# Moving the next pass's conditioning products and the home of S2 in a TensorE-filled kernel

## What is computed

```
W = weights[condition]                       # (64, 64, 64), one matrix per batch element
y = einsum('bct,bcd->bdt', x, W)             # the conditioning product
scores = y @ Wr.T                            # (4096, 64)
top_vals, top_idx = top_k(scores, 16)
G = zeros(4096, 64) with softmax(top_vals) at top_idx
h = einsum('nd,krd->nkr', y, A)              # (4096, 64, 16)
out = einsum('nkr,kdr->nd', h * G, B) * 2.0
return x + out
```

## Time and profile before

| | us |
|---|---|
| median of 3 runs | 730.85 |
| the runs | 730.23 to 731.08 |
| the profiled execution | 730.23 |
| its span in the profile | 728.4 |
| PE (TensorE matmul) busy | 714.4 (98%) |
| DVE (VectorE) busy | 490.7 (67%) |
| ACT (ScalarE) busy | 261.7 (36%) |
| POOL (GpSimd) busy | 51.0 (7%) |

### The profile page before, as it was taken

The page is one execution under the profiler, slowest core; times in us unless marked ns, Lnnn a source line. Parts: engine busy times, 40 slices in busy tenths (PEclk is TensorE's granted clock), DMA queues, the critical chain, the costliest instruction groups (busy, mean ns, idle before and its releaser), DMA issues.

```text
span 728.4 us, 9257 instructions
## 1 busy us (share of the span) xinstructions
PE 714.4 (98%) x3440; PEld 599.6 (82%) x3440; DVE 490.7 (67%) x945; ACT 261.7 (36%) x498; POOL 51.0 (7%) x38
## 2 busy tenths in 40 slices
PE   8999989999999999999999999999999999999998
PEld 7877767788888888888888888888888888888886
DVE  4598899997544787856434569875544386887742
ACT  4658662452423543222331544213222255223200
POOL 0683800000000000000000000000000000000000
PEclk9999999999999999999999999999999999999999
DMA  9949339965796956576678586746666777545663
GB/s 317 409 183 319 125 138 390 360 246 217 274 302 228 344 191 238 179 253 245 227 255 297 198 301 234 260 174 235 214 248 246 274 271 278 187 160 185 224 227 144
DMA packets 56158, 178.41 MB, mean 245 GB/s; under 512 B 9650, under 2 KB 9778, under 8 KB 55602
## 3 DMA queue, kind: packets, MB, share of 16 engines
q1 hardware_dynamic: 53954, 172.78, 65.2%
q10 hardware_dynamic: 2160, 5.05, 2.0%
HBM read 131.66 MB, written 46.14 MB: 244 GB/s over the span
## 4 chain that ended last, share of the span: by engine, by line
PE 87%; DVE 12%; ACT 0%; issue 0%; POOL 0%; DVEq 0%; POOLq 0%
PE Pb L266 40%; PE Pb L248 35%; PE Cb L228 6%; PE S L282 4%; DVE Cq L364 2%; DVE Wt L199 2%; DVE Op L181 2%; DVE R L364 1%; PE T L510 1%; DVE Xo L181 1%; DVE Q L364 1%; DVE BR L364 1%; PE T L299 0%; PE T L354 0%; DVE u L364 0%
## 5 line engine op out<-in xcount | busy, mean ns | idle before, releaser
L248 PE MATMUL Pb<-Op,Wt 128*128 128x512 f32 x1008 | 239.0, 392 | 6.9 <-DVE Op L181 5.1
L248 PEld LDWEIGHTS Pb<-Op,Wt 128*128 128x128 f32 x1008 | 187.4, 188 | 46.9 <-DVE Op L181 6.8
L266 PE MATMUL Pb<-Wt,Op 128*128 128x512 f32 x912 | 212.9, 391 | 2.6 <-DVE Op L181 2.6
L266 PEld LDWEIGHTS Pb<-Wt,Op 128*128 128x128 f32 x912 | 169.8, 188 | 38.3 <-DVE Op L181 3.9
L364 DVE TENSOR_TENSOR Q<-Pb,Q 128x512 f32<-128x512 f32 x112 | 77.4, 691 | 89.9 <-PE Pb L266 89.8
L266 PE MATMUL Pb<-Wt,Ox 128*128 128x512 f32 x432 | 100.8, 391 | 0.0
L234 ACT COPY R<-Cb 128x512 f32<-128x512 f32 x60 | 35.2, 586 | 169.5 <-PE Cb L228 169.4
L266 PEld LDWEIGHTS Pb<-Wt,Ox 128*128 128x128 f32 x432 | 80.5, 188 | 16.3
L181 DVE TENSOR_TENSOR Op<-R,Op 128x512 fp32r<-128x512 f32 x98 | 71.3, 752 | 19.0 <-ACT Op L179 19.0
L364 DVE TENSOR_TENSOR Cq<-Pb,Cq 128x512 f32<-128x512 f32 x64 | 44.1, 689 | 40.9 <-ACT Cq L375 30.9
L248 PE MATMUL Pb<-Ox,Wt 128*128 128x512 f32 x288 | 66.3, 389 | 0.0
(11 more groups left out here) (87 smaller groups left out, 482.6 us busy)
## 6 DMA issues: line engine op xcount, KB each, us to landing
Wt<-Wd SPq DMA_DIRECT2D x168, 512.0 KB, 4.8
Wd<-Wt SPq DMA_DIRECT2D x56, 512.0 KB, 3.9
Q<-in_x SPq DMA_DIRECT2D x32, 512.0 KB, 5.0
xc<-in_x SPq DMA_DIRECT2D x24, 512.0 KB, 4.4
out<-Q SPq DMA_DIRECT2D x32, 256.0 KB, 2.5
out<-Q SPq DMA_DIRECT2D x16, 512.0 KB, 2.8
BR<-in_x SPq DMA_DIRECT2D x12, 256.0 KB, 10.3
BR<-in_B SPq DMA_DIRECT2D x3, 1024.0 KB, 9.4
```

The lines of the kernel that those rows point to most:

```text
L248: t = pe.run(lambda e, c=c, o=o, a=a, z=z: e.matmul(Pb[:, b, :], Wt[:, k, a, 128 * c:128 * c + 128], part(o, z), start=fresh and (c, a, z) ...
L266: t = pe.run(lambda e, c=c, o=o, k=k, a=a, z=z: e.matmul(Pb[:, b, :], part(o, a)[:, 128 * i:128 * i + 128], Wt[:, k, z, :], start=fresh an ...
```

## The change

Three things change, all in pass 0. The tiles of the next pass's conditioning product stand behind other steps of the second half (`SPREAD`). S2 lies in `xc`, not in the upper half of `R[:, 1]`. With that the waits follow: "D" waits for the last use of the `Xo` slots, not for the earlier readers of R; the ScalarE copies of tiles 4 to 7 no longer wait for `S2_split`; and the first two loads of `xc` are issued at the steps 14 and 16 of the second half behind `S2_split`, not at the steps 24 and 26 of the first. The passes 1 to 3 keep their order.

```diff
-SPREAD = [1, 3, 4, 7, 16, 18, 20, 22]
+SPREAD = [18, 19, 21, 22, 23, 25, 26, 27]
...
-        S2x = [R[:, 1, 4 + c, :] for c in range(4)]
+        S2x = [xc[:, c // 2, 512 * (c % 2):512 * (c % 2) + 512] for c in range(4)]
...
             to = R[:, i // 4, 4 * a:4 * a + 4, 128 * (i % 4):128 * (i % 4) + 128]
-            ac.after(t, R_free[0], *(S2_split if i >= 4 else ()))
+            ac.after(t, R_free[0])
...
-                    if more and step in (24, 26):
-                        k = (step - 24) // 2
-                        if s == 0:
-                            xc_free[k] = op_free[NO + 4 + k]
-                        load_x(s + 1, k)
+                    if s and more and step in (24, 26):
+                        load_x(s + 1, (step - 24) // 2)
...
                         raw["D", j] = add(ve, s2_place(j), Cq[:, 1, j, :], Cq[:, 3, j, :], Cq_ready[1][j], Cq_ready[3][j],
-                                          *((u_busy[j],) if s else (split["y22"][j][1], t2[j], t3[j])), op=ALU.subtract)
+                                          u_busy[j] if s else op_free[NO + 4 + j // 2], op=ALU.subtract)
...
                     elif more:
                         split.setdefault("next", []).append(operand(y21[c], R_ready[0][1]))
+                    if s == 0 and step in (14, 16):
+                        xc_free[(step - 14) // 2] = S2_split[step - 13]
+                        load_x(1, (step - 14) // 2)
                     b, done = second(base + 28 + 4 * m, split[uses[m]], i, i == 3, name not in CHAIN)
```

## The result

| | before | changed |
|---|---|---|
| median, us | 730.45 (6 runs) | 736.9 (6 runs) |
| the runs, us | 729.66 to 731.08 | 736.41 to 738.64 |
| span of the profiled execution, us | 728.4 | 735.4 |
| time of the profiled execution, us | 730.23 | 737.22 |

The ratio to before is 1.0092, with a 95% interval of 1.0082 to 1.0102. 737.7 was predicted, in a range of 735.9 to 740.3.

A forecast was written before the change was run, and what follows sets the result against it. VectorE sets the pace until 152 us, TensorE after. Span 728.4 + 7.12 = 735.5 us, other terms 0; with 1.83 us around it 737.35, or 737.97 by the median. Predicted 737.7, range 735.9 to 740.3.

The forecast's parts named there:

- SPREAD, steps 0 to 8: Pass 0's second half: VectorE's times stay, TensorE waits more, step 8 restarts at 152.04 with four tiles (7.12 us) less done.
- SPREAD, steps 8 to 27: Rest of that half, at TensorE's pace with eight tiles instead of four: ends at 219.0, not 211.91; +7.12 us.
- ScalarE in the late steps: Tile copies ahead of the next splits in late steps: parts ready in time, term 0; outer end 0.5 us once.
- D's wait: First D, pass 0: new wait over beforehand, old one may have cost something; term 0, 0.4 us either way.
- Loads of xc: Late steps: median landing 5.6 us fits the 7.2 us windows of tiles 4 and 7; term 0, outer end +5.7 us.
- The signs of being wrong: S2's operand 3 over 1 us before 151.3, matmuls waiting for an xc load, or granted clock of 137 to 160 below 1.00.
- Rival (a), a hidden gain: Early steps: without tiles ScalarE runs ahead, VectorE's waits vanish, 728.2 us; 3 in 100, partial gain another 5.
- Rival (c), the clock: TensorE's clock halves for a step behind the long waits; uncovered behind 152.04, +2.7 us, 740.4; 6 in 100.

The follow-up runs named there:

- late tiles only: Kernel before with only the new SPREAD list; S2's place, D's waits and the first two xc loads kept: 737.64 us, ratio 1.0099.
- two tiles: Kernel before with two tiles in early steps (behind 3 and 7) and six in late steps: 733.63 us, ratio 1.0046.
- the filler: Changed kernel with eight useless identity matmuls behind each of the steps 1, 3, 4 and 7: 737.61 us, ratio 1.0098.
- The two D experiments: Kernel before without D's waits for earlier readers of R: 730.11 us; changed kernel with D's waits for GpSimd sums put back: 737.69 us.
- the weights above: Changed kernel with the four weight loads of step 24, pass 0's second half, held back to step 26: 737.17 us, ratio 1.0098.
- the moved sums: T2b sums moved to steps 2 to 5, T1b sums to steps 14 to 17: changed kernel 732.69 us; kernel before 729.12 us.

## Why the prediction was right

**SPREAD, steps 0 to 8: right.** VectorE's times did not move with TensorE's, and the restart of step 8 stands where it stood but for D. The pattern was as said, but the four waits come to 7.00 us where 1.25 + 9.0 was forecast, for three reasons. D's gain is in the first (0.67 for 1.25). The profile lists 0.96 us for the three matmuls in front of a wait, where I took 0.68, so each wait reads about 0.28 shorter than in my walk (2.0 and 3.1 forecast; 1.71 and 2.84 with late tiles only). And behind 135.57 the 48 matmuls took 13.08 us; at the 0.2275 us of the earlier trace rows they take 10.9, and the two waits forecast in step 8 (3.9 us) shrank to one of 1.85.

**SPREAD, steps 8 to 27: right.** +7.10 us in the kernel with this part alone, 7.12 in the sum; the slope holds for two tiles as well, and the filler shows the other side of it.

**ScalarE in the late steps: right, term 0.** VectorE waits 2.23 us for ScalarE's split behind seven of the eight tiles, as in the row at 199.47, and 3.53 behind the last, and no TensorE wait names VectorE behind 150.51.

**D's wait: the size was off.** I took 0 and allowed 0.4 either way. It was 0.66 us gained: 0.45 at the first D and 0.07 at each of the other three, where I had seen no cost. The two D experiments show it. The new wait, for Xo, cost nothing, as said: VectorE has waited for a later matmul by then, so `after` puts none into its list.

**Loads of xc: the place was right, the term was not.** The last tile, one of the two with a 7.2 us window, waited 1.06 us in one profile and 0.74 in the other; I had taken the median landing. I had not looked at the four weight loads of step 24, which stand in front of it. Whether they made it late is open (see the weights above). These two misses, -0.66 and +1.3 in the profiled execution (68.09 us from step 8 to pass 1, where the kernels without the wait have 66.8), partly cancel, so the total is closer than its terms; that is luck. The medians rose by 6.45 us, less than the terms of the profile together (7.12 - 0.66 + 1.3 = 7.8); nothing here says how much of this is a load that is late only at times and how much the spread of the runs.

**The signs of being wrong came, all three by the letter.** Matmuls waited for a load of xc, which cost some 1.3 us. The granted clock of 137 to 160 was below 1.00, at 0.50 until 139, which cost nothing. And S2's operand 3 was made from 149.76, 1.5 us before 151.3; 0.87 of this is the start of the execution and 0.66 D. The restarts forecast at 137.1 and 152.0 within 0.5 us (135.57 and 150.51) were missed by the same 1.5 us. So the signs were set too tight and in positions that differ between executions; the mechanism, tiles free in front of step 8 and paid behind it, is what the experiments show.

**Rival (a), a hidden gain: no.** With the tiles gone from the early steps step 8 came no earlier (54.72 with late tiles only, as before). What did bring it forward was on VectorE: 0.66 us by D's waits, 3.68 by the moved sums.

**Rival (c), the clock: it fell, and cost nothing.** The changed kernel's stretches (PE busy first, granted clock third from the end):

```profile
131.00:133.00 2.00, 0.97 (x3) 0.48 (x3) 2.00 (x5) 0.81 (x2) 0.00 (x0) 0.96 0.45 184
133.00:135.00 2.00, 0.00 (x0) 0.00 (x0) 1.90 (x4) 0.62 (x2) 0.00 (x0) 0.50 0.33 133
135.00:139.00 4.00, 3.43 (x8) 2.75 (x9) 3.96 (x7) 1.16 (x3) 0.00 (x0) 0.50 0.38 154
139.00:141.00 2.00, 2.00 (x8) 1.56 (x8) 2.00 (x5) 0.00 (x0) 0.00 (x0) 0.83 0.22 90
```

The clock falls to the 1.2 GHz level at about 132.8 us (0.96 as the mean of 131 to 133) and is back at about 139.7. At 132.8 the wait of 1.64 us and three matmuls lie behind it, and the wait of 2.84 us has just begun, so the long wait is not what brought it down. Step 8's wait covers the loss, as the filler shows. The fall behind step 8, the one that would have cost, did not come: 1.00 from 141 on. I had given it 6 in 100 on the strength of one row at 2.42 us; a better reading would have said that the clock may well fall and then asked what covers it.

## What to carry to other kernels

Where two engines are both near full, find which one's times don't move when the other's do: VectorE's were nearly back to back with no wait for TensorE, and that made its last operation for step 8 the fixed point of the sum. Work of the other engine in front of that point is free and behind it is paid, so filler belongs in front. To make such a stretch shorter, move what isn't due yet out of the pacing engine's list, and look at its pauses, which don't appear as work: those behind an operation whose result is needed at once, and waits long fulfilled that stand in the same place.

## What the runs showed of the hardware

**A wait that is long fulfilled can still cost VectorE time.** With the wait for GpSimd's sums the first D starts 1.16 to 1.18 us behind the start of its predecessor (five kernels), without it 0.71 to 0.74 (seven kernels), in both cases with both homes of S2. The operations around it start 0.60 us apart. One that waits for the result of the one just before it starts 0.71 to 0.73 us behind (T1b), and with a wait for GpSimd besides, 0.78 to 0.79 (T2b in its old place, the later D's). The wait for GpSimd alone costs nothing: T2b in its new place has it too, its other inputs are long there, and it starts 0.60 to 0.61 us behind in the four kernels with the sums moved. First the kernel before without D's waits, then the changed kernel with the sums moved:

```profile
121.72 0.68 DVE L199 TENSOR_TENSOR Wt<-BR,Wt 128x512 fp32r<-128x512 f32 x1
122.51 0.69 DVE L364 TENSOR_TENSOR BR<-BR 128x512 f32<-128x512 f32 x1
```
```profile
131.73 0.69 DVE L363 TENSOR_TENSOR Q<-Pb,Q 128x512 f32<-128x512 f32 x1
132.33 0.69 DVE L363 TENSOR_TENSOR BR<-BR 128x512 f32<-128x512 f32 x1
```

Why the first D's wait costs 0.45 and the next ones 0.07 is open. That it comes first is not enough: without D's waits the first T2b is the first operation in this stretch that waits for GpSimd, and it pays 0.07 like the others.

**The clock falls at shorter waits than one that it survives.** The 2.42 us wait at 97.32 left it at 1.00, and so did a wait of 2.37 us in front of step 8's last chunk with late tiles only (1.00 from 152 to 219). The changed kernel with the sums moved has one wait of 2.18 us behind 11 us of matmuls, and TensorE is at the half level behind it:

```profile
134.88 12.76 PE L265 MATMUL Pb<-Wt,Op 128*128 128x512 f32 x48 [2.18 <-DVE Op L180]
```
```profile
135.00:137.00 2.00, 2.00 (x5) 1.57 (x6) 2.00 (x4) 0.29 (x1) 0.00 (x0) 0.51 0.39 158
137.00:139.00 2.00, 2.00 (x7) 1.56 (x6) 2.00 (x5) 0.85 (x2) 0.00 (x0) 0.64 0.48 193
```

The Trainium skill, "TensorE: Matmul & The Clock Gate", section "Why this matters for your kernels", puts the danger at idle gaps of more than about 3 us. Here the clock fell behind a single gap of 2.18 us, and in the changed kernel behind one of 1.64 us and three matmuls, and the measurement decides. What else than the length of the gap decides is not shown.
